# Graph attention with a residual layer norm: negative sums with both halves side by side, halves added on GpSimd

## The reference

```python
h = jnp.einsum('bnf,hfo->bhno', x, W)
s1 = jnp.einsum('bhno,ho->bhn', h, a1)
s2 = jnp.einsum('bhno,ho->bhn', h, a2)
e = jax.nn.leaky_relu(s1[..., :, None] + s2[..., None, :], negative_slope=0.2)
attn = jax.nn.softmax(jnp.where((adj > 0)[:, None], e, NEG_INF), axis=-1)
h_prime = jnp.einsum('bhnm,bhmo->bhno', attn, h)      # heads side by side again
x = layernorm(x + h_prime)
```

## Time and profile before

| what | value |
|---|---|
| median of three runs | 2842.45 us |
| the profiled execution | 2844.84 us, span 2843.1 us |
| TensorE matmul busy | 2667.5 us (94%), weight load 2313.9 us (81%) |
| VectorE busy | 2491.9 us (88%) |
| ScalarE busy | 2333.0 us (82%) |
| GpSimd busy | 1236.4 us (43%) |
| mean granted TensorE clock | 0.978 |

### The profile page before, as it was taken

One profiled execution on the slowest core, in us unless ns is written; L12 is line 12 of the kernel. 1 busy time (PEld: TensorE's weight loads), 2 busy tenths in 40 slices (PEclk: granted clock), 3 DMA queues, 4 the chain that ended last, 5 costly groups with the idle time before them and its releaser, 6 DMA issues.

```text
span 2843.1 us, 126766 instructions
## 1 busy us (share of the span) xinstructions
PE 2667.5 (94%) x52546; PEld 2313.9 (81%) x52546; DVE 2491.9 (88%) x3836; ACT 2333.0 (82%) x3886; POOL 1236.4 (43%) x1011
## 2 busy tenths in 40 slices
PE   6899999999999999999999999999999999999996
PEld 3499876999679986799958999499984999859986
DVE  6799988889898998999889998889988999889996
ACT  4599974999659997599957998489983999839994
POOL 4544436434354434544354443544436444264442
PEclk9999999999999999999999999999999999999998
DMA  6456643676535765277553775447754477546773
GB/s 186 101 132 166 164 127 90 135 167 154 137 78 140 173 148 146 69 151 177 136 135 76 175 171 133 117 99 170 168 122 115 113 165 167 124 107 127 165 169 94
DMA packets 281214, 390.33 MB, mean 137 GB/s; under 512 B 161857, under 2 KB 161857, under 8 KB 280673
## 3 DMA queue, kind: packets, MB, share of 16 engines
q1 hardware_dynamic: 253536, 315.24, 42.5%
q0 software_dynamic: 27136, 67.12, 14.4%
HBM read 313.52 MB, written 34.14 MB: 122 GB/s over the span
## 4 chain that ended last, share of the span: by engine, by line
PE 53%; ACT 22%; issue 9%; DVE 9%; DMA 3%; POOL 2%; SPq 1%; DVEq 0%; ACTq 0%; POOLq 0%
ACT m_pos L630 19%; PE ps L549 18%; PE ps L518 10%; PE ps L583 10%; PE ps L584 10%; ACT adj_cut L595 2%; DMA y<-in_x 1%; PE ps L429 1%; PE ps L466 1%; DVE m_pos L849 1%; DMA adj_in<-in_adj 1%; PE ps L448 1%; PE ps L479 1%; DVE m_pos L835 1%; DVE prod L818 1%
## 5 line engine op out<-in xcount | busy, mean ns | idle before, releaser
L630 ACT ACTIVATE m_pos<-ps,s_steep 128x512 fp8e4<-128x512 f32 x3432 | 2063.0, 952 | 119.6 <-DVE s_neg L789 62.8
L583 PE MATMUL ps<-d_hi,m_neg 128*128 128x65 f16 x16384 | 1081.1, 194 | 19.2 <-issue 18.8
L584 PE MATMUL ps<-d_lo,m_neg 128*128 128x65 f16 x16384 | 1079.2, 194 | 14.0 <-issue 13.5
L584 PEld LDWEIGHTS ps<-d_lo,m_neg 128*128 128x128 fp8e5 x16384 | 1028.1, 98 | 62.9 <-issue 31.2
L549 PE MATMUL ps<-b_both,m_pos 128*128 128x130 f16 x16384 | 1016.6, 221 | 53.9 <-DVE total L692 20.3
L583 PEld LDWEIGHTS ps<-d_hi,m_neg 128*128 128x128 fp8e5 x16384 | 1043.4, 98 | 18.3 <-issue 18.0
L549 PEld LDWEIGHTS ps<-b_both,m_pos 128*128 128x128 fp8e5 x16384 | 962.2, 98 | 63.4 <-issue 62.5
L1011 POOL TENSOR_TENSOR den_scaled<-den_inv,bound 128x4 f32<-128x4 f32 x256 | 506.5, 1979 | 1120.9 <-DVE den_inv L703 1104.8
L849 DVE TENSOR_TENSOR m_pos<-m_pos,maskT 128x1024 uint32<-128x1024 uint32 x512 | 620.1, 1228 | 146.8 <-ACT m_pos L630 145.2
L856 DVE TENSOR_TENSOR m_neg<-m_pos,maskT 128x2048 uint32<-128x2048 uint32 x256 | 586.6, 2291 | 1.1
L518 PE MATMUL ps<-W_sb,xT 128*128 128x512 f32 x1024 | 455.0, 605 | 32.6 <-issue 20.9
(11 more groups left out here) (94 smaller groups left out, 1563.5 us busy)
## 6 DMA issues: line engine op xcount, KB each, us to landing
adj_in<-in_adj SPq DMA_DIRECT2D x266, 512.0 KB, 4.7
s_bc<-s_rows SPq DMA_DIRECT2D x258, 256.0 KB, 3.6
x_in<-in_x SPq DMA_DIRECT2D x134, 256.0 KB, 4.4
x_sum<-in_x POOLq DMA_DIRECT2D x128, 256.0 KB, 4.9
y<-in_x POOLq DMA_DIRECT2D x32, 1024.0 KB, 9.8
out<-y SPq DMA_DIRECT2D x32, 1024.0 KB, 6.6
maskT<-adj_cut SPq DMA_TRANSPOSE x264, 4.1
m_neg<-in_x SPq DMA_DIRECT2D x10, 256.0 KB, 3.1
```

Source lines behind the costliest of these rows:

```text
L583: pe.matmul(acc, mask, d_hi[:, j, h, :], start=(j == 0), stop=False)
L584: mm = pe.matmul(acc, mask, d_lo[:, j, h, :], start=False, stop=(j == JC - 1))
L630: ins = nc.scalar.activation(chunk(m_pos[unit % 3], j, 0, BLK), ps[:, BANK_S1 + unit % 2, :], ACT.Relu, bias=s2_steep[:, j, h:h + 1], scal ...
```

## The change

The negative sums take the form of the positive ones: d_hi and d_lo become the two halves of d_both, one matmul of 130 columns takes both, and the result of four tiles fills banks 2 and 3. So every unit uses the same pair of banks, and the wait on neg_read before the negative sums is now for the unit directly before. VectorE only scales the result (128x520) into neg_part; GpSimd adds both halves to total, takes the power of minus one of the last column, and then scales and multiplies as before. neg_part has one buffer: the product of a unit waits until both additions of the unit before are done. The last four chunks of the projection use banks 6 and 7 by turns. In unit 0 the order on TensorE is: chunks 0 to 11 of the positive side, 0 to 12 of the negative side, the rest of the positive side, the spread of s1 for unit 3, the turning of an x tile, the rest of the negative side.

```diff
-    H_BANKS = (7, 6, 2)
+    H_BANKS = (7, 6, 3) * (JC // 4) + (6, 7, 6, 7)
+    POS_FIRST, NEG_FIRST = 12, 13
-        d_hi = sb("d_hi", [P, JC, H, O1], F16)
-        d_lo = sb("d_lo", [P, JC, H, O1], F16)
+        d_both = sb("d_both", [P, JC, H, 2, O1], F16)
+        d_hi, d_lo = d_both[:, :, :, 0, :], d_both[:, :, :, 1, :]
-        neg_part = sb("neg_part", [P, IT, O1], F32)
+        neg_part = sb("neg_part", [P, IT, 2 * O1], F32)
...
+            def add_neg(h, tiles, first, last):
+                for it in tiles:
+                    acc = neg_slots()[:, it, :]
+                    for j in range(first, last):
+                        mask = chunk(m_neg[h % 2], j, it * P, P).bitcast(FP8_WIDE)
+                        mm = pe.matmul(acc, mask, d_both[:, j, h, :, :], start=(j == 0 and it % 2 == 0),
+                                       stop=(j == JC - 1 and it % 2 == 1))
+                return mm
...
-                        pe.wait_ge(neg_read, at(neg_read, b * UNITS - 1))
+                        pe.wait_ge(neg_read, at(neg_read, b * UNITS))
...
-                        pe.wait_ge(neg_read, at(neg_read, u - 1))
+                        pe.wait_ge(neg_read, at(neg_read, u))
...
-                V.tensor_tensor(neg_part[:], neg, r, ALU.mult).then_inc(neg_read, 1)
-                dve.wait_ge(neg_read, at(neg_read, u + 1))
-                V.tensor_tensor(total[hp][:], total[hp][:], neg_part[:], ALU.add).then_inc(total_made, 1)
-                dve.wait_ge(total_made, u + 1)
-                V.reciprocal(den_inv[hp][:], total[hp][:, :, O]).then_inc(den_inverted, 1)
+                dve.wait_ge(total_made, at(total_made, 2 * u))
+                V.tensor_tensor(neg_part[:], neg_slots(), r, ALU.mult).then_inc(neg_read, 1)
...
             def divide_unit(u, h, g, par):
+                pool.wait_ge(pos_read, at(pos_read, u + 1))
+                pool.wait_ge(neg_read, at(neg_read, u + 1))
+                for part in range(2):
+                    G.tensor_tensor(total[hp][:], total[hp][:], neg_part[:, :, part * O1:(part + 1) * O1], ALU.add).then_inc(total_made, 1)
+                    pool.wait_ge(total_made, at(total_made, 2 * u + part + 1))
+                G.tensor_tensor(den[hp][:], total[hp][:, :, O], minus_one[:], ALU.pow).then_inc(den_inverted, 1)
                 pool.wait_ge(den_inverted, u + 1)
-                G.tensor_tensor(den_scaled[hp][:], den_inv[hp][:], bound[:].to_broadcast([P, IT]), ALU.mult
+                G.tensor_tensor(den_scaled[hp][:], den[hp][:], bound[:].to_broadcast([P, IT]), ALU.mult
```

More of the change, by code:

```diff
@@ L569, in _ @@
                         pe.sem_inc(waited[pe.engine], 1)
[L570 removed]
+                        pe.wait_ge(neg_read, at(neg_read, u))
                         pe.sem_inc(waited[pe.engine], 1)
[L572 to L584 removed]
+                        add_neg(h, range(IT // 2), 0, JC)
+                        if unit < UNITS - 3:
+                            spread_s1(unit + 3, u + 3)
+                        if unit >= UNITS - 2:
+                            if unit == UNITS - 2:
+                                pe.wait_ge(s1_T_copied, b + 2)
+                            spread_s1(unit + 2 - UNITS, u + 2)
+                        mm = add_neg(h, range(IT // 2, IT), 0, JC)
                         mm.then_inc(unit_done, 1)
```

91 lines of the change are left out of this document (51 added, 40 removed).

## The result

The changed kernel takes 2866.2 us (median of 4 runs, 2862.2 to 2869.0) against 2841.2 us for the kernel before (4 runs beside it, 2840.0 to 2843.4): ratio 1.008, 95% interval 1.006 to 1.010. It is slower by 25 us where I forecast 6 us faster. The traces show 21.7 us of it inside the span; the rest lies outside: an execution takes 4.2 to 4.5 us more than its span in the changed kernel and 1.7 in the profiled run before, which my sum carried over unchanged.

A forecast was written before the change was run, and what follows sets the result against it. TensorE was taken as the bound, with ScalarE close to it as a second. Terms of -22 (middle), -27 (unit 0), +34 and +2 (tail and final divide) and +6 (block 0) gave -7 us, so 2835 us; range 2790 to 2890.

The forecast's parts named there:

- The middle: Unit 3's to unit 30's comparison in each batch: falls from 240.0 to 237.2 us, eight times, -22 us.
- hidden: GpSimd's added work per unit: chain of 5.7 to 7.5 us, under a unit's 8.1 to 8.9, costs nothing between units.
- The tail: Last units of a batch: additions wait behind GpSimd's all_reduce, +4.2 us, seven times and at the end, +34, plus 2.
- D: Time zero of the tail: the start of total for unit 28; units to end 32.0 us later, 27.8 before.
- Unit 0: Start of each batch, new TensorE order: ScalarE starts 8.3 us after it, mean 11.7 before; -3.3, eight times, -27.
- The ring: Projection chunks 14 and 15 wait for VectorE's products of nearer chunks: 0 us taken, 0.7 as the other end.
- Block 0's 0.7 a batch: First block of each batch, where VectorE has little spare: GpSimd's added work costs 0.7 us, eight times, +6.
- rival 3: GpSimd's additions and y hold VectorE's m_pos or comparison, up to 0.61 us each: about 2910 us; chance 0.20.
- the port: SBUF ports of VectorE and GpSimd, kept by whichever starts first: the mechanism of rival 3, about 2910 us, chance 0.20.

The follow-up runs named there:

- e14: The changed kernel with only the load of s1 moved behind the unit's adjacency pieces on SyncE's queue; 2824.6 us, ratio 0.994.
- e7: The changed kernel with unit 0's old order on TensorE restored, pairing and single bank pair kept; 2885.4 us, ratio 1.018.
- e11: e8 with the projection's chunks 12 to 15 in banks 2, 7, 6, 7 instead of 6, 7, 6, 7; 2804.1 us, ratio 0.986.
- e10: e8 with GpSimd's two additions cut to the denominator column, 4 of 260 elements each; 2821.8 us, ratio 0.992.
- e8: The changed kernel with adjacency loads ahead on SyncE's queue and the additions of units 28 to 31 on VectorE; 2806.2 us, ratio 0.990.
- e15: The changed kernel with s1's load behind the adjacency pieces, units 28 to 31's additions on VectorE, projection chunks 12 to 15 in banks 2, 7, 6, 7; 2793.8 us, 0.986.
- e3: The changed kernel with both additions and a reciprocal of all units on VectorE instead of GpSimd; 2917.9 us, ratio 1.027.

## Why the prediction was wrong

1. **The middle** is the step that failed. I wrote that TensorE "sheds 0.33 us a unit until it stands there, and then goes at ScalarE's pace", with "some 237.2 of it is work". The first half held: TensorE waits 128 times for the product (176.4 us) and ScalarE hardly for the spread (3.3 us in the eight middles, 21.8 before). But ScalarE's pace was not its work. In place of the spread it met late adjacency loads (39.9 us, 6.1 before), and the stretch stayed at 240.5. Rows for those loads were not among those that I read: SyncE's queue does not show in a count of busy time, and before the change the loads for units 9, 17 and 25 landed just in time. I had also called GpSimd's longer chain "hidden" between units; it is for VectorE, but it moves GpSimd's own transfers, which now overlap with these loads. With the supply mended (e14) the middle is 235.55, 4.5 us a batch less than in the kernel before, more than my 2.8, since ScalarE's work is 235 us and not 237.2: I had left idle times of under a microsecond in it.
2. **The tail**: mechanism right, size a little off. GpSimd came free at D + 18.65, not 17.0: the all_reduce starts 1.0 later as forecast, its record is 1.3 us longer (1.75 against 0.42) and the hold behind it 8.10 instead of 7.75. So the idle time was 5.34, not 3.7, and the units ended at D + 34.6, not D + 32.0. Of the delay, 1.15 us came back, since TensorE's issue time at the projection fell from 3.00 to 1.85. In all +34.4 for seven batches against 29.4. At the end +9.0 against 6.2.
3. **Unit 0**: -29.0 against -27, 8.05 us against 8.3. As an account of cause it was too generous: by the stage of e7 the order alone is worth 18.
4. **The ring** (the banks of the projection's last chunks): I took 0 with 0.7 as the other end. It was 3.5 us in this pair of traces, in the first batch alone (projection to unit 0: 66.5 to 69.2 us in four traces with the old banks, 70.9 to 75.2 in ten with the changed ones, 66.4 to 67.2 in the five with e11's), because chunk 12 and not only 14 and 15 came to wait for a nearer chunk, and there VectorE stands 9.3 us for s1. Seven batches showed nothing.
5. **Block 0's 0.7 a batch and rival 3**: the lengthening is there (comparisons 552 ns against 483, m_pos 1253 against 1228), and m_neg held GpSimd's first addition as forecast (3.43 us for a pair, 1.44 free). The Trainium skill (SBUF — State Buffer, Who interferes with whom) describes this lock in both directions for VectorE instructions with two SBUF inputs, as those that write m_pos and m_neg; by that rule, the trace agrees, and even additions of 4 elements take 2.46 us a pair behind m_neg in e10. The part of it that e10 took away had no price that could be measured; the rest was not tested.
6. The chances: the stages that I had priced as separate were separate (e8: the gains add; in e15 only the stages show it). What was missing was a rival for the middle in which the freed engine meets another supply. Missing too was a term for the 2.5 us outside the span. I had given 0.36 to slower, most of it by the port, which was not the reason.

## What to carry to other kernels

When an edit frees the engine that paces, look up who supplies it next, transfers first: for every load, what its issuing queue waits for ahead of it. A wait placed ahead of an unrelated load on the same queue costs nothing while the load still lands in time; look how much time is to spare, for here it was none. Work moved to a side engine is paid where that engine has its one long instruction, so keep it off there (four units of 32); and it moves the transfers that this engine issues.

## What the runs showed of the hardware

- Inside a batch GpSimd's all_reduce holds the engine far longer than its record: 0.42 to 2.38 us recorded, 6.8 to 9.8 us from its end to the next instruction, over all traces. The first one, before the batches, has 1.47 us behind it.
- TensorE after 5.34 us without a matmul ran 32 matmuls 107 ns apart, at a granted clock of 0.50, and the next 58 ns apart, at 0.99: the level of 1.2 GHz, then that of 2.4.
- An adjacency load of 512 KB took 4.5 us from issue to landing in unit 17 before and 7.0 after, where in all eight batches one of GpSimd's transfers (256 KB, accumulating) was in flight beside it for 6.6 us; that the one lengthens the other is an inference.
- With 16384 fewer matmuls, TensorE's idle times put down to issue fell from 49 to 2.6 us outside the projection, and from 20.9 to 12.7 at its seven starts; that is in none of my terms. It is not settled by the number of matmuls alone: with as many as the changed kernel, e14 has 11.4 us outside the projection and e10 27.3.
- A second VectorE addition of 260 elements right behind the first is cheap (0.89 us for the pair), yet 1.3 us more a unit on VectorE cost 8 us a batch in e3, most of it as ScalarE's waits for loads that SyncE issues behind VectorE's comparison.
